# Line recurrences of a two-layer image kernel: even and odd column pairs in two halves of 96 dense rows

## The chip, the cores and the metric

The kernel runs on one core of one Trainium2 chip. The metric is the device time of one launch in microseconds (us). A core has a matrix engine (PE, whose loads of the stationary operand are listed apart as PEld), a vector engine (DVE), a scalar engine (ACT), GpSimd (POOL), a queue engine (SP) and 16 DMA engines. Every engine works its own list of instructions in order and waits on semaphores.

## What is computed

The input x is (2, 48, 512, 512) in float32. Layer 0 adds a convolution with channel attention, layer 1 adds four recurrences over lines of the normalized image:

```python
def step(w, b):
    def f(carry, inp):
        nxt = inp + _conv1d(carry, w, b)      # 48 -> 48 channels, K = 5 taps along the line, padding 2
        return (nxt, nxt)
    return f
_, d_rest = scan(step(down_w, down_b), xs[0], xs[1:])       # D: rows downwards
seq = concatenate([D[Hh - 3::-1], D[Hh - 1:Hh]], 0)
_, u_rest = scan(step(down_w, down_b), D[Hh - 1], seq)      # U: rows upwards
_, r_rest = scan(step(right_w, right_b), ws[0], ws[1:])     # R: columns of U to the right
_, l_rest = scan(step(left_w, left_b), R[Ww - 1], R[Ww - 2::-1])   # L: columns of R to the left
x = x + L
```

Each recurrence has 512 lines, and a line needs the one before it. So there are 4 x 512 = 2,048 dependent steps, each a convolution of 48 channels with 5 taps over 512 places, for a batch of two.

## The kernel before

Layer 0 and the statistics of the second normalization take the first half of the time; the change leaves them alone but for the small preparation of weights in `split_scan_taps`. Then `scans` (L1146) runs the four ways "down", "up", "right", "left" one after the other, and `final_sum` adds the result to x.

**Layout.** The 512 places of a line are taken as 256 pairs. A tile has 112 partitions: the 48 channels of the even places in rows 0 to 47, those of the odd places in rows 64 to 111, and 16 rows of zeros between. The free axis holds 2 batches x 256 pairs = 512 columns (`LP`). The five taps become three 112 x 112 matrices, for the pair before, the pair itself and the pair after; a shift by one pair is a shift of the 512 columns by one, and `hi` and `lo` have an empty column at each end of a batch.

**Precision.** A state is kept as a sum hi + lo of two fp32r tiles, and the taps as scan_high + scan_low. A line needs scan_high x hi, scan_low x hi and scan_high x lo, three shifts each: nine matmuls of 512 columns. The fourth product is left out.

**One line k** (`steps` of each engine):
- the line's input plus bias is written into one of `SLOTS` = 4 PSUM banks ahead of time (`seed`): ACT does it in "down" (two ACTIVATEs, one per batch, L1567) and "right" (L1571, read with a stride of 16 floats), DVE in "up" and "left" (L1472);
- PE adds the three scan_high x hi passes of line k (`high_products`, L1401) and counts `conv_done`;
- ACT casts the bank into `hi` (L1588) and counts `hi_ready`, which PE needs for the next line's first products;
- PE meanwhile adds the three scan_low x hi passes (`low_products`, L1409) and, once `lo` of the line before is there, the three scan_high x lo passes (L1414), and counts `low_done`;
- DVE computes lo = bank - hi (L1483), waiting for `low_done` and for the state two lines back;
- POOL adds hi + lo (L1520) into the tile that goes to memory in "down" and "right", or into a ring of 16 lines in "up" and "left" (`room`); from the ring ACT copies four lines at a time into the transposed layout of the leaving tile (`lay`: L1544 in "up", two copies in most lines, L1538 in "left").

PE's order within a line is high products of line k + 1, then low products of line k. ACT's and DVE's order is written out in their `steps`: the line's own operation, then a seed or copies.

**Transfers.** Groups of T = 16 lines are loaded and stored by SP, double buffered. A load of group g waits until the seeds have read group g - 2 (`consumed`), a store until the states (or the copies out of the ring) of the group are complete. In "down" SP issues all four loads of a group; ACT issues two of the first four. POOL clears the 32 rows between the parities of the first two input tiles (L1523) before the first loads of "down".

## Time and profile before

| | us |
|---|---|
| median of 3 runs | 10,179.8 (10,179.77 to 10,181.08) |
| the profiled execution | 10,184.16 |
| its span, first to last instruction | 10,182.5 |
| PE busy | 9,178.7 (90%) |
| PE weight loads busy | 7,753.5 (76%) |
| DVE busy | 6,163.4 (61%) |
| ACT busy | 6,540.9 (64%) |
| POOL busy | 2,811.9 (28%) |
| granted PE clock, mean over the span | 0.957 of full speed |

Matmuls are pipelined and their records overlap, so that a busy PE need not be one at its peak: the distance from start to start tells more. A row of a timeline gives the start, the length, the engine, the line of the kernel, the operation with what it writes and reads, the shape and the number of instructions merged into it, and in brackets how long the engine had been idle and what ended that. "SPq" and "ACTq" are the issue of transfers.

### The profile page before, as it was taken

What the parts mean: (1) busy time and instruction counts of PE and PEld (TensorE: products, weight loads), DVE (VectorE), ACT (ScalarE), POOL (GpSimd) and SP (SyncE); (2) the same over time, 40 slices, a digit from 0 to 9 for tenths busy, and PEclk for the clock granted to TensorE, in tenths of its full rate; (3) what the DMA queues carried; (4) which work ended last, traced back from release to release, by engine and by line L of the source; (5) the groups of instructions that cost most, each with busy time, mean ns of one, the idle gap of its engine ahead of it and who ended that gap; (6) DMA issues with size and microseconds to landing.
All of it is one profiled execution on the core that took longest, in us unless ns stands there. A gap on an engine that the chain in (4) does not pass through costs nothing. (4 is left out here: it accounts for less than half of the span.)

```text
span 10182.5 us, 167735 instructions
## 1 busy us (share of the span) xinstructions
PE 9178.7 (90%) x53872; PEld 7753.5 (76%) x53872; DVE 6163.4 (61%) x10420; ACT 6540.9 (64%) x10026; POOL 2811.9 (28%) x2287
## 2 busy tenths in 40 slices
PE   3999999999999999999899999999999999999000
PEld 3999999999999998777677777777777777777000
DVE  8888888777777775666633335666433336666323
ACT  2777777777777775444377777888877775555000
POOL 0000000000000000000156665666566656666000
PEclk9999999999999999999999999999999999999555
DMA  8888887666666665999989986777766657777999
GB/s 268 171 166 170 170 169 145 129 132 131 134 135 132 133 135 132 291 291 287 257 182 206 198 206 184 218 218 217 206 223 212 220 180 203 203 202 190 371 433 408
DMA packets 770594, 2101.18 MB, mean 206 GB/s; under 512 B 58976, under 2 KB 633728, under 8 KB 674256
## 3 DMA queue, kind: packets, MB, share of 16 engines
q1 hardware_dynamic: 629824, 1744.21, 67.0%
q0 software_dynamic: 34304, 151.01, 5.8%
q10 hardware_dynamic: 106368, 204.76, 5.6%
q8 instruction: 48, 0.79, 0.0%
q14 instruction: 50, 0.41, 0.0%
HBM read 1344.55 MB, written 754.97 MB: 206 GB/s over the span
## 5 line engine op out<-in xcount | busy, mean ns | idle before, releaser
L1483 DVE TENSOR_TENSOR lo<-scan_ps,hi 112x512 fp32r<-112x512 f32 x2048 | 1416.1, 691 | 2263.0 <-PE scan_ps L1414 1130.7
L1588 ACT CAST hi<-scan_ps 112x512 fp32r<-112x512 f32 x2048 | 1202.9, 587 | 1095.5 <-PE scan_ps L1401 1082.7
L463 PE MATMUL conv_ps<-tap_low,x_high 128*128 128x432 f32 (+2 forms) x6144 | 1904.9, 310 | 0.0
L463 PE MATMUL conv_ps<-tap_high,x_low 128*128 128x432 f32 (+2 forms) x6144 | 1903.6, 310 | 0.0
L463 PE MATMUL conv_ps<-tap_high,x_high 128*128 128x432 f32 (+2 forms) x6144 | 1881.0, 306 | 13.0 <-DVE x_edge L659 7.5
L1401 PE MATMUL scan_ps<-hi,scan_high 112*112 112x512 f32 x6132 | 1777.4, 398 | 40.4 <-ACT hi L1588 33.0
L1414 PE MATMUL scan_ps<-lo,scan_high 112*112 112x512 f32 x6132 | 1769.8, 397 | 0.6
L1409 PE MATMUL scan_ps<-hi,scan_low 112*112 112x512 f32 x6132 | 1768.2, 397 | 0.0
L1520 POOL TENSOR_TENSOR lines<-hi,lo 112x512 f32<-112x512 f32 x1024 | 1323.0, 1292 | 871.4 <-DVE lo L1483 871.4
L1520 POOL TENSOR_TENSOR ring<-hi,lo 112x512 f32<-112x512 f32 x1024 | 1326.2, 1295 | 843.9 <-DVE lo L1483 843.9
L1401 PEld LDWEIGHTS scan_ps<-hi,scan_high 112*112 112x112 f32 x6132 | 1075.4, 176 | 408.6 <-ACT scan_ps L1567 18.0
L1414 PEld LDWEIGHTS scan_ps<-lo,scan_high 112*112 112x112 f32 x6132 | 1077.2, 176 | 365.9 <-DVE lo L1483 3.6
L1409 PEld LDWEIGHTS scan_ps<-hi,scan_low 112*112 112x112 f32 x6132 | 1076.6, 176 | 361.9
L310 ACT ACTIVATE x_high<-raw,negmean 128x512 fp32r<-128x512 f32 x1024 | 1208.1, 1232 | 11.7 <-DMA v_blocks<-xs 6.9
L655 DVE SCALAR_TENSOR_TENSOR x_low<-raw,negmean,x_high 128x512 fp32r<-128x512 f32 x1024 | 1147.3, 1150 | 85.1 <-ACT x_high L310 85.0
L463 PEld LDWEIGHTS conv_ps<-tap_high,x_high 128*128 128x128 f32 x6144 | 1160.8, 189 | 35.4 <-issue 9.1
L463 PEld LDWEIGHTS conv_ps<-tap_high,x_low 128*128 128x128 f32 x6144 | 1164.4, 190 | 18.8
L463 PEld LDWEIGHTS conv_ps<-tap_low,x_high 128*128 128x128 f32 x6144 | 1162.2, 189 | 19.9 <-issue 0.2
L351 ACT COPY xs<-conv_ps 128x288 f32<-128x288 f32 x1024 | 409.4, 400 | 975.2 <-PE conv_ps L469 974.0
L670 DVE TENSOR_TENSOR xs<-conv_ps,xs 128x192 f32<-128x192 f32 x1024 | 365.1, 357 | 657.3 <-ACT vt L352 651.8
L1472 DVE TENSOR_SCALAR scan_ps<-lines,scan_bias 112x512 f32<-112x512 f32 x1021 | 760.6, 745 | 0.0
L1544 ACT COPY lines<-ring 48x512 f32<-48x512 f32 x1024 | 669.4, 654 | 19.3 <-POOL ring L1520 0.9
(145 smaller groups left out, 11670.0 us busy)
## 6 DMA issues: line engine op xcount, KB each, us to landing
raw<-x SPq DMA_DIRECT2D x764, 256.0 KB, 4.9
d_rows<-lines SPq DMA_DIRECT2D x32, 3584.0 KB, 24.3
u_cols<-lines SPq DMA_DIRECT2D x64, 1792.0 KB, 10.6
r_cols<-lines SPq DMA_DIRECT2D x32, 3584.0 KB, 16.6
lines<-u_cols SPq DMA_DIRECT2D x31, 3584.0 KB, 16.4
lines<-r_cols SPq DMA_DIRECT2D x30, 3584.0 KB, 16.6
lines<-d_rows SPq DMA_DIRECT2D x30, 3360.0 KB, 15.5
v_blocks<-xs ACTq DMA_DIRECT2D x128, 768.0 KB, 4.5
```

Of the source, the lines that this page charges most:

```text
L310: ins = nc.scalar.activation(x_high[:, s, k, :, 1:TOK + 1], phases(raw, s, k), ACT.Identity, bias=negmean0[:, 0, b:b + 1], scale=1.0)
L351: nc.scalar.copy(qk_at(i % 2, dy, 0, 3), qk_of(left))
L463: nc.tensor.matmul(bank(dy, side, lo - side, hi - side), xs[at], ws[taps], start=fresh[side], stop=False, skip_group_check=True)
L655: ins = nc.vector.scalar_tensor_tensor(x_low[:, s, k, :, 1:TOK + 1], phases(raw, s, k), negmean0[:, 0, b:b + 1], x_high[:, s, k, :, 1:TOK ...
L1401: last = nc.tensor.matmul(slot(k), w_hi[:, TAPS_OF[way], shift], hi[:, (k - 1) % HIS, :, shift:shift + LP], start=False, stop=False, skip_ ...
L1409: nc.tensor.matmul(slot(k), w_lo[:, TAPS_OF[way], shift], hi[:, (k - 1) % HIS, :, shift:shift + LP], start=False, stop=False, skip_group_c ...
L1414: last = nc.tensor.matmul(slot(k), w_hi[:, TAPS_OF[way], shift], lo[:, (k - 1) % LOS, :, shift:shift + LP], start=False, stop=shift == 2, ...
L1472: ins = nc.vector.tensor_scalar(to, of, b_sb[:, TAPS_OF[way]:TAPS_OF[way] + 1], None, ALU.add)
L1483: nc.vector.tensor_tensor(low_of(k), ps[:, k % SLOTS], high_of(k), ALU.subtract).then_inc(lo_ready, 1)
L1520: nc.gpsimd.tensor_tensor(state(way, s, k), high_of(k), low_of(k), ALU.add).then_inc(state_done, 1)
L1544: return nc.scalar.copy(tile[ODD * r:ODD * r + C, b, h:h + LEAD // 2, :, :, q], rows.rearrange("p t (c m) -> p t c m", c=W // T))
L1588: nc.scalar.copy(high_of(k), ps[:, k % SLOTS]).then_inc(hi_ready, 1)
```

## The change

Even and odd places still lie in one tile, but densely: rows 0 to 47 and 48 to 95 (`SC` = 96). The pairs of a line are now themselves split: even pairs form the half X and odd pairs the half Y of the free axis, 2 batches x 128 pairs (`LQ`) = 256 columns each. The middle tap matrix takes a whole line in one pass for the scan_high x hi product; the neighbours need half passes, since the pair before an even pair is an odd one. Rows 96 to 127 are free: `hi` gets there, in its X half, a copy of rows 32 to 63 of the Y half (made by ACT), and `lo` gets copies of rows 0 to 31 and 64 to 95 of hi's Y half in its Y and X halves (made by DVE, two copies a line). The weight tiles have matching rows of scan_low, so that passes over 128 rows carry part of the scan_low x hi product along with others. A line now has 15 matmuls: 1 of 512 columns and 4 of 256 for the high product, 4 of 256 before the wait for `lo` and 6 of 256 behind it.

Every way is seeded by both engines, DVE batch 1 and ACT batch 0, into 8 PSUM banks. The ring and ACT's copies out of it are gone: POOL writes the leaving tile directly, in "up" in runs of four floats, in "left" one float in every 32. The memsets of rows 32 to 63 go. SP's loads wait for `hi_ready` instead of the seeds, the stores of "up" are four transfers instead of two, and ACT issues half of the loads of "down" (`load_down`). Tensors in memory have 96 rows instead of 112.

```diff
-        scan_high = keep("scan_high", [PP, len(weights), 3, PP], F32R)
-        scan_low = keep("scan_low", [PP, len(weights), 3, PP], F32R)
-        scan_bias = keep("scan_bias", [PP, len(weights)])
+        scan_high = keep("scan_high", [128, len(weights), 4, SC], F32R)
+        scan_low = keep("scan_low", [128, len(weights), 3, SC], F32R)
...
-                        link(nc.vector.tensor_copy(scan_high[:], scan_taps[:]))
-                        nc.vector.tensor_tensor(scan_low[:], scan_taps[:], scan_high[:], ALU.subtract)
+                        rows, spare = slice(0, SC), slice(SC, 128)
+                        nc.vector.tensor_copy(scan_high[rows, :, 3], scan_taps[:, :, 1])
+                        link(nc.vector.tensor_copy(scan_high[rows, :, 0:3], scan_taps[:]))
+                        link(nc.vector.tensor_tensor(scan_low[rows], scan_taps[:], scan_high[rows, :, 0:3], ALU.subtract))
+                        for tile, at, first, shift in ((scan_low, 0, 32, 1), (scan_low, 1, 32, 2), (scan_high, 0, 64, 1),
+                                                       (scan_high, 1, 64, 2), (scan_high, 2, 0, 2), (scan_high, 3, 0, 1)):
+                            nc.vector.tensor_copy(tile[spare, :, at], scan_low[first:first + 32, :, shift])
...
-    LP = W2
-    RING = 16
-    LEAD = 4
+    LQ = W2 // 2
+    ROWS, SPARE = slice(0, SC), slice(SC, 128)
+    X, Y = 0, 1
...
-    DVE_AHEAD = 3
-    HIS, LOS, SLOTS = 4, 2, 4
+    DVE_AHEAD = 4
+    HIS, LOS, SLOTS = 4, 2, 8
...
+    ACT_SEEDS, DVE_SEEDS = 0, 1
...
-    STORES = {"down": 1, "up": 2, "right": 1, "left": 4}
+    STORES = {"down": 1, "up": 4, "right": 1, "left": 4}
...
-        lines = [sb(f"lines{n}", [PP, 2, T * B * LP]) for n in range(2)]
...
-        hi = sb("hi", [PP, HIS, B, LP + 2], F32R)
-        lo = sb("lo", [PP, LOS, B, LP + 2], F32R)
-        ring = sb("ring", [PP, RING, B, LP])
...
+        lines = [sb(f"lines{n}", [SC, 2, T * B * W2]) for n in range(2)]
+        skipped = sb("skipped", [SC, B * W2])
+        hi = sb("hi", [128, HIS, 2, B, LQ + 2], F32R)
+        lo = sb("lo", [128, LOS, 2, B, LQ + 2], F32R)
...
+        banks = ctx.enter_context(nc.psum_tensor("scan_ps", [PP, SLOTS, 2, B, LQ], F32))
+        ps = banks[ROWS]
...
+        def spare_of(tile, x):
+            return tile[SPARE, x, :, 1:LQ + 1]
+        def odd_rows(k, at):
+            return hi[at:at + 128 - SC, k % HIS, Y, :, 1:LQ + 1]
...
-                    sp.wait_ge(seeded[way], seeds0(way) + T * g - T)
+                    sp.wait_ge(hi_ready, states0(way) + T * g - T)
+                def written(way, g):
+                    sp.wait_ge(state_done, states0(way) + T * g + T)
...
                 def store_up(g, s):
-                    for b in range(B):
-                        tile = leaving("up", s).rearrange("p (b c x) -> p b c x", b=B, c=W // T)[:, b]
-                        sp.dma_start(u_cols[:, :, b, bass.ds(g * -NP + NP * (G - 1), NP)].rearrange("c p h t -> p c (h t)"),
-                                     tile).then_inc(stored["up"][s], 16)
+                    for q in range(2):
+                        tile = leaving("up", s)[C * q:C * q + C].rearrange("p (r c n) -> p r c n", r=2, c=W // T)
+                        for r in range(2):
+                            sp.dma_start(u_cols[:, r, :, q, bass.ds(g * -1 + (G - 1), 1)].rearrange("g c u n -> c g (u n)"),
+                                         tile[:, r]).then_inc(stored["up"][s], 16)
...
-                def slot(k):
-                    return ps[:, k % SLOTS]
+                def half(way, k, x, taps, at, of, x_in, shift, rows=ROWS):
+                    return nc.tensor.matmul(ps[:, k % SLOTS, x], taps[rows, TAPS_OF[way], at], of[rows, x_in, :, shift:shift + LQ],
+                                            start=False, stop=False, skip_group_check=True)
...
                 def high_products(way, g, k):
-                    pe.wait_ge(seeded[way], seeds0(way) + T * g + k + 1)
+                    high = hi[:, (k - 1) % HIS]
+                    await_seeds(pe, way, T * g + k + 1)
                     pe.wait_ge(hi_ready, states0(way) + T * g + k)
-                    for shift in range(3):
-                        last = nc.tensor.matmul(slot(k), w_hi[:, TAPS_OF[way], shift], hi[:, (k - 1) % HIS, :, shift:shift + LP],
-                                                start=False, stop=False, skip_group_check=True)
-                    last.then_inc(conv_done, 1)
+                    nc.tensor.matmul(ps[:, k % SLOTS], w_hi[ROWS, TAPS_OF[way], 1], high[ROWS, :, :, 1:LQ + 1],
+                                     start=False, stop=False, skip_group_check=True)
+                    half(way, k, X, w_hi, 0, high, Y, 0)
+                    half(way, k, Y, w_hi, 0, high, X, 1)
+                    half(way, k, X, w_hi, 2, high, Y, 1)
+                    half(way, k, Y, w_hi, 2, high, X, 2).then_inc(conv_done, 1)
                 def low_products(way, g, k):
+                    high, low, every = hi[:, (k - 1) % HIS], lo[:, (k - 1) % LOS], slice(0, 128)
                     pe.wait_ge(hi_ready, states0(way) + T * g + k + 1)
-                    for shift in range(3):
-                        nc.tensor.matmul(slot(k), w_lo[:, TAPS_OF[way], shift], hi[:, (k - 1) % HIS, :, shift:shift + LP],
-                                         start=False, stop=False, skip_group_check=True)
+                    half(way, k, Y, w_lo, 0, high, X, 1, every)
+                    half(way, k, X, w_lo, 0, high, Y, 0)
+                    half(way, k, X, w_lo, 1, high, X, 1, every)
+                    half(way, k, Y, w_lo, 2, high, X, 2)
                     pe.wait_ge(lo_ready, states0(way) + T * g + k)
-                    for shift in range(3):
-                        last = nc.tensor.matmul(slot(k), w_hi[:, TAPS_OF[way], shift], lo[:, (k - 1) % LOS, :, shift:shift + LP],
-                                                start=False, stop=shift == 2, skip_group_check=True)
-                    last.then_inc(low_done, 1)
+                    half(way, k, Y, w_hi, 0, low, X, 1, every)
+                    half(way, k, X, w_hi, 0, low, Y, 0)
+                    half(way, k, X, w_hi, 1, low, X, 1, every)
+                    half(way, k, Y, w_hi, 3, low, Y, 1, every)
+                    half(way, k, X, w_hi, 2, low, Y, 1, every)
+                    half(way, k, Y, w_hi, 2, low, X, 2).then_inc(low_done, 1)
...
                     slot_free(v, way, g - s, k, kept)
-                    to, of = ps[:, k % SLOTS], line(way, s, k % T, kept)
-                    if bare:
+                    b = DVE_SEEDS
+                    to, of = ps[:, k % SLOTS, :, b], line(way, s, k % T, b, kept)
+                    if way == "down":
+                        shift = gn1_bias if bare else down_shift
+                        ins = nc.vector.tensor_scalar(to, of, gn1_scale[:, b:b + 1], shift[:, b:b + 1], ALU.mult, ALU.add)
+                    elif bare:
                         ins = nc.vector.tensor_copy(to, of)
                     else:
                         ins = nc.vector.tensor_scalar(to, of, b_sb[:, TAPS_OF[way]:TAPS_OF[way] + 1], None, ALU.add)
-                    ins.then_inc(dve_seeded, 1)
+                    ins.then_inc(dve_seeded[way], 1)
                 def steps(way, g, first=False, last=False):
                     for k in range(2 * T):
                         done = states0(way) + T * g + k
                         v.wait_ge(hi_ready, done + 1)
+                        nc.vector.tensor_copy(spare_of(lo[:, k % LOS], Y), odd_rows(k, 0))
+                        nc.vector.tensor_copy(spare_of(lo[:, k % LOS], X), odd_rows(k, 64))
                         if not (first and k == 0):
                             v.wait_ge(low_done, convs0(way) + T * g + k)
                         if not (way == "down" and first and k < LOS):
                             v.wait_ge(state_done, done - LOS + 1)
                         nc.vector.tensor_tensor(low_of(k), ps[:, k % SLOTS], high_of(k), ALU.subtract).then_inc(lo_ready, 1)
-                        if way in laid:
...
+                        ahead = k + DVE_AHEAD
+                        if ahead < 2 * T:
+                            seed(way, g + ahead // T, ahead // T, ahead, first)
+                        elif not last:
+                            seed(way, g + ahead // T, ahead // T - 2, ahead - 2 * T)
...
+                def state(way, s, k):
+                    high, low = high_of(k), low_of(k)
+                    if way == "up":
+                        r, h = (T - 1 - k % T) % 2, (T - 1 - k % T) // 2
+                        tile = leaving(way, s).rearrange("p (r c h x b m) -> p r h (x b) c m", r=2, c=W // T, h=NP, x=2, b=B)
+                        return (tile[:, r, h], high.rearrange("p x b (c m) -> p (x b) c m", c=W // T),
+                                low.rearrange("p x b (c m) -> p (x b) c m", c=W // T))
+                    if way == "left":
+                        tile = leaving(way, s).rearrange("p (b m x t) -> p x b m t", b=B, x=2, t=T)
+                        return tile[..., T - 1 - k % T], high, low
+                    return leaving(way, s).rearrange("p (t x b m) -> p t x b m", t=T, x=2, b=B)[:, k % T], high, low
...
-                        nc.gpsimd.tensor_tensor(state(way, s, k), high_of(k), low_of(k), ALU.add).then_inc(state_done, 1)
-                for s in range(2):
-                    nc.gpsimd.memset(arriving("down", s)[32:64], 0.0).then_inc(between_clear, 1)
...
                     arrived(act, way, g, s, k % T, kept)
-                    slot_free(act, way, g - s, k, kept)
-                    to, of = ps[:, k % SLOTS], line(way, s, k % T, kept)
+                    act.wait_ge(dve_seeded[way], T * (g - s) + k + 1)
+                    b = ACT_SEEDS
+                    to, of = ps[:, k % SLOTS, :, b], line(way, s, k % T, b, kept)
...
-                        for b in range(B):
-                            ins = nc.scalar.activation(to[:, b], of[:, b], ACT.Identity, bias=shift[:, b:b + 1], scale=gn1_scale[:, b:b + 1])
+                        ins = nc.scalar.activation(to, of, ACT.Identity, bias=shift[:, b:b + 1], scale=gn1_scale[:, b:b + 1])
...
-                def behind(way, g, k):
...
-                        if way in laid:
-                            if not (first and k < LEAD + LAG):
-                                behind(way, g, k)
-                        else:
-                            ahead = k + ACT_AHEAD
-                            if ahead < 2 * T:
-                                seed(way, g + ahead // T, ahead // T, ahead, first)
-                            elif not last:
-                                seed(way, g + ahead // T, ahead // T - 2, ahead - 2 * T)
...
+                        if way == "down" and k == LAG and not first:
+                            await_seeds(act, way, T * g)
+                            load_down(act, g + 1, 1, 1)
+                        if way == "down" and k == T + LAG and not last:
+                            await_seeds(act, way, T * g + T)
+                            load_down(act, g + 2, 0, 1)
+                        ahead = k + ACT_AHEAD
+                        if ahead < 2 * T:
+                            seed(way, g + ahead // T, ahead // T, ahead, first)
+                        elif not last:
+                            seed(way, g + ahead // T, ahead // T - 2, ahead - 2 * T)
+                        act.wait_ge(hi_ready, states0(way) + T * g + k + 1)
+                        nc.scalar.copy(spare_of(hi[:, k % HIS], X), odd_rows(k, 32))
```

## Rows read from the trace of the kernel before

**Rows 1.** The page's part 1: busy us (share) and instructions of each engine.

```profile
PE 9178.7 (90%) x53872; PEld 7753.5 (76%) x53872; DVE 6163.4 (61%) x10420; ACT 6540.9 (64%) x10026; POOL 2811.9 (28%) x2287
```

**Rows 2.** Windows: one stretch of each way. Busy of PE, PEld, DVE, ACT, POOL; PEclk; DMA; GB/s.

```profile
5101.00:6136.00 1035.00, 1035.00 (x4416) 773.65 (x4415) 339.30 (x491) 757.31 (x1470) 633.00 (x490) 1.00 0.89 198
...
```

**Rows 3.** Timeline of "right", one line and the start of the next.

```profile
7500.13 0.69 DVE L1483 TENSOR_TENSOR lo<-scan_ps,hi 112x512 fp32r<-112x512 f32 x1 [1.42 <-PE scan_ps L1414]
...
7500.58 0.86 PE L1409 MATMUL scan_ps<-hi,scan_low 112*112 112x512 f32 x3
7500.78 0.59 ACT L1588 CAST hi<-scan_ps 112x512 fp32r<-112x512 f32 x1 [0.47 <-PE scan_ps L1401]
7500.97 1.29 POOL L1520 TENSOR_TENSOR lines<-hi,lo 112x512 f32<-112x512 f32 x1 [0.81 <-DVE lo L1483]
...
7502.69 0.86 PE L1409 MATMUL scan_ps<-hi,scan_low 112*112 112x512 f32 x3
```

**Rows 4.** Timeline of PE in the first layer: 288 and 144 columns wide.

```profile
2500.83 0.29 PE L463 MATMUL conv_ps<-tap_low,x_high 128*128 128x288 f32 x1
2500.96 0.29 PE L463 MATMUL conv_ps<-tap_high,x_low 128*128 128x288 f32 x1
...
2501.16 0.28 PE L463 MATMUL conv_ps<-tap_low,x_high 128*128 128x144 f32 x1
2501.27 0.27 PE L463 MATMUL conv_ps<-tap_high,x_low 128*128 128x144 f32 x1
```

**Rows 5.** Groups by line: busy us, mean ns | idle before, releaser.

```profile
L1472 DVE TENSOR_SCALAR scan_ps<-lines,scan_bias 112x512 f32<-112x512 f32 x1021 | 760.6, 745 | 0.0
...
L1544 ACT COPY lines<-ring 48x512 f32<-48x512 f32 x1024 | 669.4, 654 | 19.3 <-POOL ring L1520 0.9
L1571 ACT ACTIVATE scan_ps<-lines,scan_bias 112x512 f32<-112x512 f32 x511 | 593.2, 1161 | 0.0
L1567 ACT ACTIVATE scan_ps<-lines,down_shift,gn_scale 112x256 f32<-112x256 f32 x1022 | 543.3, 567 | 0.0
...
L1569 ACT COPY scan_ps<-lines 112x512 f32<-112x512 f32 x1 | 1.0, 1014 | 2.6 <-DMA lines<-lines 2.6
```

**Rows 6.** Timeline of SP's queue: loads of "down", a store of "up".

```profile
5226.96 2.08 SPq L1263 DMA_DIRECT2D lines<-x_scan  x4
...
6498.77 4.82 SPq L1302 DMA_DIRECT2D u_cols<-lines  x1
```

**Rows 7.** Timelines at 3,961 us and 5,067 us: DVE beside POOL's memsets.

```profile
3961.54 6.91 POOL L865 MEMSET res<- 112x8192 f32 x1
...
3964.49 0.17 DVE L99 TENSOR_TENSOR rnorm<-rnorm,norm 96x16 f32<-96x16 f32 x1
...
3964.90 3.58 DVE L101 TENSOR_SCALAR rnorm<-rnorm 96x16 f32<-96x16 f32 x1
...
5067.13 13.80 POOL L1523 MEMSET lines<- 32x8192 f32 x2 [12.70 <-POOLq L811]
5067.17 6.90 DVE L1449 COPY gn_mean<-x_mv 112x2 f32<-112x2 f32 x1 [3.96 <-PEq L811]
```

**Rows 8.** Groups: DVE from SBUF to SBUF, one input.

```profile
L647 DVE COPY raw<-mean 32x512 f32<-32x512 f32 x2 | 0.8, 420 | 0.1
...
L597 DVE CAST edge_high<-edge_f 128x288 fp32r<-128x288 f32 x2 | 0.6, 302 | 0.0
```

**Rows 9.** Timeline of "up": DVE's two operations of a line and POOL's.

```profile
6499.68 0.69 DVE L1483 TENSOR_TENSOR lo<-scan_ps,hi 112x512 fp32r<-112x512 f32 x1 [0.75 <-issue]
...
6500.29 0.74 DVE L1472 TENSOR_SCALAR scan_ps<-lines,scan_bias 112x512 f32<-112x512 f32 x1
...
6500.52 1.29 POOL L1520 TENSOR_TENSOR ring<-hi,lo 112x512 f32<-112x512 f32 x1 [0.81 <-DVE lo L1483]
```

**Rows 10.** Timeline of PE in the first lines of "down", at the lower clock.

```profile
5100.25 1.48 PE L1414 MATMUL scan_ps<-lo,scan_high 112*112 112x512 f32 x3
...
5101.53 1.41 PE L1401 MATMUL scan_ps<-hi,scan_high 112*112 112x512 f32 x3
```

More of the change, by code:

```diff
@@ L24 @@
 PP = ODD + C
+SC = 2 * C
 T = 16
@@ L1186, in scans @@
         hi_ready, state_done, lo_ready = sem("hi_ready"), sem("state_done"), sem("lo_ready")
-        act_seeded, dve_seeded = sem("act_seeded"), sem("dve_seeded")
-        seeded = {"down": act_seeded, "up": dve_seeded, "right": act_seeded, "left": dve_seeded}
+        act_seeded = {way: sem(f"{way}_act_seeded") for way in WAYS}
+        dve_seeded = {way: sem(f"{way}_dve_seeded") for way in WAYS}
         loaded = {way: [sem(f"{way}_loaded{s}") for s in range(2)] for way in WAYS}
         stored = {way: [sem(f"{way}_stored{s}") for s in range(2)] for way in WAYS}
-        laid = {way: sem(f"{way}_laid") for way in ("up", "left")}
         skipped_in, first_right = sem("skipped_in"), sem("first_right")
@@ L1254, in slot_free, with await_seeds @@
                 engine.wait_ge(lo_ready, states0(way) + T * g + k - SLOTS + 1)
+        def await_seeds(engine, way, n):
+            engine.wait_ge(act_seeded[way], n)
+            engine.wait_ge(dve_seeded[way], n)
         def high_free(engine, way, g, k, first):
@@ L1273, in load_up @@
                 def load_up(g, s, last=False):
-                    rows = arriving("up", s).rearrange("p (t x) -> p t x", t=T)
-                    here = one(d_rows, g * -1 + (G - 1)).rearrange("g p t b n -> (g p) t (b n)")
-                    before = one(d_rows, G - 1 if last else g * -1 + (G - 2)).rearrange("g p t b n -> (g p) t (b n)")
+                    rows = arriving("up", s).rearrange("p (t n) -> p t n", t=T)
+                    here = one(d_rows, g * -1 + (G - 1)).rearrange("g p t n -> (g p) t n")
+                    before = one(d_rows, G - 1 if last else g * -1 + (G - 2)).rearrange("g p t n -> (g p) t n")
                     sp.dma_start(rows[:, 1:T], here[:, 0:T - 1]).then_inc(loaded["up"][s], 16)
@@ L1334, in _ @@
                         consumed("down", 2 * i + s)
-                        for q in range(2):
-                            load_down(sp, 2 * i + s, s, q)
+                        load_down(sp, 2 * i + s, s, 0)
                         store_rows("down", d_rows, 2 * i + s - 2, s)
@@ L1503, in room @@
                 def room(way, g, s, k, kept):
-                    if way in laid:
-                        if k % LEAD == 0 and not (kept and T * s + k < RING):
-                            pool.wait_ge(laid[way], (T // LEAD) * g + k // LEAD - (RING // LEAD - 1))
-                    elif k == 0:
+                    if k == 0:
                         if not kept:
@@ L1547, in lay_block @@
-                def lay_block(way, g, s, k, at, of):
-                    n_ops = 8 if way == "up" else 4
-                    if at == 0 and k == 0 and not (isinstance(g, int) and g < 2):
-                        act.wait_ge(stored[way][s], 8 * STORES[way] * (g - s))
-                    if at == 0:
-                        act.wait_ge(state_done, states0(way) + T * g + k + LEAD)
-                    for j in range((n_ops * at + of - 1) // of, (n_ops * (at + 1) + of - 1) // of):
-                        ins = lay(way, s, k, j)
-                        if j == n_ops - 1:
-                            ins.then_inc(laid[way], 1)
@@ L1571, in seed @@
                         ins = nc.scalar.activation(to, of, ACT.Identity, bias=b_sb[:, TAPS_OF[way]:TAPS_OF[way] + 1], scale=1.0)
-                    ins.then_inc(act_seeded, 1)
-                def behind(way, g, k):
-                    at = k - LAG - LEAD - (k - LAG) % LEAD
-                    gone, s = (g + at // T, at // T) if at >= 0 else (g - 1, 1)
-                    for half in range(2):
-                        lay_block(way, gone, s, at % T, 2 * ((k - LAG) % LEAD) + half, 2 * LEAD)
+                    ins.then_inc(act_seeded[way], 1)
                 def steps(way, g, first=False, last=False):
@@ L1583, in steps @@
                         if first and k == 0:
[L1584 removed]
+                            await_seeds(act, way, 1)
                         else:
@@ L1607, in _ @@
                 for way in WAYS:
-                    if way not in laid:
-                        if way == "right":
-                            act.wait_ge(first_right, 16 * FIRST_RIGHT)
-                        for k in range(ACT_AHEAD):
-                            seed(way, 0, 0, k, True, k == 0)
+                    if way == "right":
+                        act.wait_ge(first_right, 16 * FIRST_RIGHT)
+                    elif way in ("up", "left"):
+                        act.wait_ge(state_done, states0(way))
+                    for k in range(ACT_AHEAD):
+                        seed(way, 0, 0, k, True, k == 0)
                     steps(way, 0, first=True)
@@ L1616, in _ @@
                     steps(way, G - 2, last=True)
-                    if way in laid:
-                        for k in range(2 * T, 2 * T + LEAD + LAG):
-                            behind(way, G - 2, k)
 def final_sum(nc, sem, x1_scan, l_rows, out):
```

153 lines of the change are left out of this document (67 added, 86 removed).

## The prediction

> **What bounds the kernel now.** I read the engine totals first, then busy time by stage, then one line of a recurrence in order of time, then the waits. The totals [rows 1] have PE at 90%; matmuls overlap in the records, so the stages are needed. The four recurrences run one after the other, and in each PE is busy throughout at a granted clock of 0.99 to 1.00, the 2.4 GHz level (the row of the first; the other three read the same to within 2%) [rows 2]. There are 2,048 lines. In the timeline of "right" the three L1409 passes of one line start at 7500.58 and those of the next at 7502.69: **2.11 us a line**, nine passes, 0.234 us each, with no gap at the three places where PE waits [rows 3]. 2,048 x 2.11 = 4,321 us, the stage's length. In the same rows each other engine waits within the line: ACT 0.47 us, DVE 1.42, POOL 0.81. So PE's stream sets the line. What follows, the final sum, is not touched.
>
> **What PE gains.** Per line 9 full passes (18 halves) become 1 full and 14 half passes: 16 halves in 15 matmuls. No 256-wide matmul stands in the trace; its neighbours do. In the first layer 288-wide passes start 0.13 us apart and 144-wide ones 0.11 us apart, both with 128-column weights [rows 4]. So the interval follows the width (288 wide 0.13, 512 wide 0.234: both 0.457 ns a column) until about 0.11 us, where the weight load takes over. 256 x 0.457 = 0.117 us is above that floor, and the new weights have 96 columns, not 128. I take 0.117 (ends 0.117 and 0.13); the line is 16 x 0.117 = **1.875 us** of PE, 0.235 less. The whole saving, if nothing else ends later: 0.235 x 2,048 = 481 us.
>
> **What ACT gets.** The cast stays, 0.59 us [rows 3]. In "down" its two seeds of 256 columns become one, 0.567. In "up" and "left" the copies out of the ring go (L1544, 0.654 each, two in most lines of "up" [rows 5]) and a seed comes; in "right" a seed of 512 halves. The strided 512-wide seed took 1.161 [rows 5], so a strided 256-wide one lies between 0.567 and 0.72. The new copy into the 32 spare rows of hi costs between 0.33, half of the 512-wide copy L1544, and 0.567, the 256-wide seed with its two scalars; I take 0.40. Sum 1.56 to 1.71 us, under 1.875: no cost, though only 0.2 us covers it. ACT also issues two transfers in 16 lines of "down", which SP did in 0.52 us each (four in 2.08) [rows 6]: 1 us a group, in ACT's idle time if the line is as long as I forecast, otherwise at most 30 us over the 32 groups.
>
> **What DVE gets.** Its subtraction stays at 0.69 [rows 3]. A seed of 512 columns took 0.745 [rows 5]; with 0.17 us of it fixed (the small L99 [rows 7]) the half is 0.46. In "down" and "right" it is new. New in every line are two copies, 32 rows x 256, SBUF to SBUF. Rows for such copies: 288 wide in 0.302, 512 wide in 0.420 [rows 8], so 0.5 ns a column and 256 wide 0.286 each. That is twice the subtraction's and the seed's pace (the seed: 0.575 us for 512, 1.1 ns a column). Alone, DVE has 0.69 + 0.46 + 0.57 = 1.72 us, again under 1.875.
>
> **The step that decides.** Those two copies stand on DVE's queue between the seed and the next subtraction, and POOL's addition of the line (1.29 us) begins 0.15 us after each subtraction ends (7500.82 to 7500.97 [rows 3]) and lasts until 1.44 us after it. Twice the trace of before shows a plain one-source f32 DVE operation from SBUF to SBUF beginning while POOL runs [rows 7]. L1449 copies two columns: 6.903 us, from 5067.17 to 5074.07, while POOL's first memset (half of 13.80) ends at 5074.03. L101 scales 16 columns: 3.58 us from 3964.90, ending at 3968.48, while the memset L865 ends at 3968.45. L99, of the same size but with two inputs, ran just before it beside the same memset in 0.17, and in the recurrence the seed, which writes PSUM, runs at 0.74 beside POOL's addition [rows 9]. So the fast copy from SBUF to SBUF waits for POOL and the others don't. That is how I take the new copies: blocked until POOL's addition ends.
> Then the line is a loop DVE, POOL, DVE: lag 0.15 + POOL 1.29 + copies + subtraction 0.69. A blocked operation ended 0.03 to 0.04 us after POOL (its start-up is past), so the first copy needs 0.03 + 0.13 (256 columns at 0.5 ns) = 0.16 after POOL; the second 0.286; hand-over 0.03: 0.15 + 1.29 + 0.16 + 0.286 + 0.03 + 0.69 = **2.60 us**. Lower end 2.415, with each of the two later operations beginning 0.08 us before the last one ends, as seed and subtraction do [rows 9]; upper end 2.80, where the first copy has its full 0.286 behind POOL with 0.04 gaps. Behind a subtraction PE has a lag (POOL's was 0.15), 6 + 6 + 4 half passes, 0.15 + 0.70 + 0.70 + 0.47 = 2.02 us, and then waits some 0.6 us for the next remainder.
> The Trainium skill ("SBUF — State Buffer", "Who interferes with whom") has the rule: a DVE copy in a two-port mode and a GpSimd instruction hold one shared pair of SBUF ports exclusively, and the second one fully blocks. The trace agrees for memsets (the two rows above); beside a POOL addition no row of before has such a copy. Without the rule the sum would be rival 1's.
>
> **Small terms.** POOL's writes in "up" come in runs of four floats, in "left" one every 128 bytes. No POOL row is strided. On ACT a copy with a 64-byte stride took 1.014 us (L1569) against 0.654 (L1544) [rows 5], 1.55 times, and against the cast's 0.59 1.7 times; POOL by that 2.0 to 2.14. POOL spends 2.5 ns an element (1.29 / 512) where the cast spends 1.15, so it has time for a slow write and I take nothing and keep +0.85 us x 512 = +435 us for "left" as an end. The two memsets ahead of "down" go: the first load waits for one of them, 6.9 us [rows 7], so -7 us. SP issues four stores in a group of "up" instead of two (4.82 us for one [rows 6]): at most 19 us in a group of over 30, and the same bytes less 1/7. Its loads now wait for the cast, not the seed, two to three lines later, and still come 12 lines, over 22 us, ahead of the first seed that reads them. The six copies that fill the spare weight rows come once, at the start; by the 0.302 of a 288-wide one [rows 8] they are 2 us.
>
> **Sum.** (2.60 - 2.11) x 2,048 = +1,004; -7; on the profiled execution's 10,184.2: 11,181. The median of the runs is 4 us lower; I forecast **11,180 us**. Own range of this case: 2.415 gives +625, 10,800; 2.80 gives +1,413, 11,590, with the strided end 12,025.
>
> **Rivals.**
> 1. *The copies don't wait* (POOL's additions, unlike memsets, leave the ports free, or the order differs). PE stays the bound at 1.875 us: 10,180 - 481 - 7 + 30 = **9,720 us**. For it: each engine fits, DVE with 0.15 us to spare. Against it: both blocked rows. It ends on the other side, and decides from the point where the two copies together take less than 0.72 us (1.875 - 0.69 - 0.46) beside POOL. Chance 0.15.
> 2. *The copies go at half the pace, like the seed, and don't wait*: about 0.42 each (0.286 + 0.133); DVE then is the bound at 0.69 + 0.46 + 0.84 = 1.99 us. 10,180 - 0.12 x 2,048 = **9,930 us**. Against it: both rows at 0.5 ns a column, a cast into fp32r among them [rows 8]. Chance 0.10.
> 3. *No block, but strided writes slow POOL* to 2.29 us a line in "up" and "left": -0.235 x 1,024 + 0.18 x 1,024 - 7 = **10,116 us**. Chance 0.03.
> 4. *Block, and the PE clock falls* because PE pauses 0.6 us each line. At 1.2 GHz a full pass takes 0.427 us (L1414 at 5100.25 to L1401 at 5101.53 [rows 10]); 16 halves are 3.4 us, **12,840 us**. Against it: the waits are short. Chance 0.04.
>
> **How the numbers follow.** Forecast 0.68; rivals 0.15, 0.10, 0.03, 0.04. Slower by over 0.2% (20 us, about what a measurement tells from no change): 0.68 + 0.04 = 0.72. Faster: 0.15 + 0.10 + 0.02 = 0.27; same 0.01. The range from 9,700 to 11,900 takes in the forecast but for its strided tail (0.63) and rivals 1 to 3 (0.28).
>
> **What would show it.** The two new DVE copies: if blocked, the first averages near 1.2 us and ends within 0.2 of POOL's end, the second 0.29; the L1401 group waits for lo about 0.6 us a line, and the period is 2.6 in all four ways. If the copies average 0.29 beside POOL and PE starts half passes 0.117 us apart without gaps, rival 1 is right. If they average 0.42, rival 2. POOL's mean by way (1.29 or near 2) settles the strided writes, the granted clock rival 4. A 96-row pass at over 0.13 us, or the first copy ending long before POOL, would make the prediction wrong.

## The result and the profile after

The changed kernel takes **11,161.3 us** (median of 4 runs, 11,159.0 to 11,166.9) against 10,180.4 of the kernel before (also 4 runs): 1.0964 times as long, interval 1.0945 to 1.0983. It is 981 us slower. The forecast was 11,180 us. The profiled execution took 11,163.2 us, 979 more than that of before.

The engine totals of the changed kernel's page, in the columns of [rows 1]:

```profile
PE 9281.8 (83%) x66142; PEld 8312.0 (74%) x66142; DVE 9261.1 (83%) x15547; ACT 6486.3 (58%) x11050; POOL 2802.6 (25%) x2285
```

DVE grew from 6,163 to 9,261 us of busy time, POOL stayed as it was. Busy time by stretch, one of each of the four ways ("down", "up", "right", "left"), in the columns of [rows 2]:

```profile
5200.00:6200.00 1000.00, 834.03 (x5793) 712.91 (x5792) 977.30 (x1545) 605.43 (x1159) 499.39 (x387) 1.00 0.55 151
6700.00:7700.00 1000.00, 833.10 (x5794) 713.40 (x5795) 977.47 (x1547) 564.09 (x1159) 498.99 (x387) 1.00 0.62 151
7900.00:8900.00 1000.00, 830.96 (x5790) 711.95 (x5790) 977.63 (x1545) 662.94 (x1158) 499.57 (x386) 1.00 0.52 151
9200.00:10300.00 1100.00, 912.93 (x6351) 781.53 (x6350) 1075.36 (x1695) 618.72 (x1271) 551.31 (x424) 1.00 0.62 151
```

POOL makes one addition a line: 387 in 1,000 us is a line every **2.59 us**, the same in all four ways, where before it was 2.11 [rows 3]. (2.59 - 2.11) x 2,048 = 983 us, which is the whole difference. PE is no longer busy throughout (83%), the granted clock stays 1.00, and DVE shows 98%. That figure alone would read as "DVE has too much work". The timeline of one line in "down" shows otherwise (start, duration, engine, line, operation, and in brackets the idle time before it and what ended it; the two copies are L1504 and L1505, the subtraction L1510, the seed L1493, POOL's addition L1560):

```profile
5501.19 0.69 DVE L1510 TENSOR_TENSOR lo<-scan_ps,hi 96x512 fp32r<-96x512 f32 x1
5501.80 0.53 DVE L1493 TENSOR_SCALAR scan_ps<-lines,gn_scale,down_shift 96x256 f32<-96x256 f32 x1
...
5501.94 0.97 PE L1404 MATMUL scan_ps<-lo,scan_high 128*96 128x256 f32 x6 [0.44 <-DVE lo L1510]
5502.02 1.30 POOL L1560 TENSOR_TENSOR lines<-hi,lo 96x512 f32<-96x512 f32 x1 [1.30 <-DVE lo L1510]
5502.37 1.11 DVE L1504 CAST lo<-hi 32x256 fp32r<-32x256 f32 x1
...
5503.49 0.29 DVE L1505 CAST lo<-hi 32x256 fp32r<-32x256 f32 x1
...
5503.79 0.69 DVE L1510 TENSOR_TENSOR lo<-scan_ps,hi 96x512 fp32r<-96x512 f32 x1
```

Two copies of the same form, one straight after the other, take 1.11 and 0.29 us. POOL's addition runs from 5502.02 to 5503.32; the first copy starts inside it and ends at 5503.48, 0.16 after it. The next subtraction starts at 5503.79, 2.60 us after the last. It is so in nearly every line: 2,030 of the 2,048 first copies begin during POOL's addition, and they end 0.15 us behind it on average (nearly all between 0.14 and 0.16). The groups by line (busy us, mean ns of one | idle before, releaser) agree:

```profile
L1560 POOL TENSOR_TENSOR lines<-hi,lo 96x512 f32<-96x512 f32 x2048 | 2653.2, 1295 | 2708.5 <-DVE lo L1510 2704.5 <-ACT hi L1591 4.0
L1504 DVE CAST lo<-hi 32x256 fp32r<-32x256 f32 x2048 | 2237.5, 1093 | 67.4 <-ACT hi L1591 3.8
L1404 PE MATMUL scan_ps<-lo,scan_high 128*96 128x256 f32 x8176 | 1717.3, 301 | 881.5 <-DVE lo L1510 881.5
L1510 DVE TENSOR_TENSOR lo<-scan_ps,hi 96x512 fp32r<-96x512 f32 x2048 | 1406.3, 687 | 39.9 <-PE scan_ps L1404 12.3
L1604 ACT CAST hi<-hi 32x256 fp32r<-32x256 f32 x2048 | 826.0, 403 | 50.7
L1505 DVE CAST lo<-hi 32x256 fp32r<-32x256 f32 x2048 | 602.8, 294 | 27.8
```

Three engines hand the work round: POOL's idle time is ended by the subtraction (2,704 us), PE's too (881 us), and DVE shows almost none, because a blocked copy counts as busy.

### The profile page after: what moved, and what is told of

Same layout as the page of the kernel before. It is cut to its first block and busy times, and to the rows that moved or that the text cites. A ratio compares the mean times of both kernels' runs of the same rounds, so it can differ in the third digit from the quotient of the medians.

```text
span 11161.6 us, 201419 instructions
## 1 busy us (share of the span) xinstructions
PE 9281.8 (83%) x66142; PEld 8312.0 (74%) x66142; DVE 9261.1 (83%) x15547; ACT 6486.3 (58%) x11050; POOL 2802.6 (25%) x2285
## 5 line engine op out<-in xcount | busy, mean ns | idle before, releaser
L1560 POOL TENSOR_TENSOR lines<-hi,lo 96x512 f32<-96x512 f32 x2048 | 2653.2, 1295 | 2708.5 <-DVE lo L1510 2704.5
L1404 PE MATMUL scan_ps<-lo,scan_high 128*96 128x256 f32 x12264 | 1965.6, 295 | 881.5 <-DVE lo L1510 881.5
L1404 PEld LDWEIGHTS scan_ps<-lo,scan_high 128*96 128x96 f32 x12264 | 1480.7, 162 | 1355.9 <-DVE lo L1510 1354.9
L1504 DVE CAST lo<-hi 32x256 fp32r<-32x256 f32 x2048 | 2237.5, 1093 | 67.4 <-ACT hi L1591 3.8
L1591 ACT CAST hi<-scan_ps 96x512 fp32r<-96x512 f32 x2048 | 1193.1, 583 | 595.9 <-PE scan_ps L1404 587.4
L1510 DVE TENSOR_TENSOR lo<-scan_ps,hi 96x512 fp32r<-96x512 f32 x2048 | 1406.3, 687 | 39.9 <-PE scan_ps L1404 12.3
L1404 PE MATMUL scan_ps<-hi,scan_low 128*96 128x256 f32 x8176 | 1315.1, 282 | 0.0
L1404 PE MATMUL scan_ps<-hi,scan_high 96*96 96x256 f32 x8176 | 1313.4, 282 | 0.0
L1404 PEld LDWEIGHTS scan_ps<-hi,scan_high 96*96 96x96 f32 x8176 | 1152.5, 162 | 155.4
L1404 PEld LDWEIGHTS scan_ps<-hi,scan_low 128*96 128x96 f32 x8176 | 1072.8, 163 | 0.0
```

Source lines behind the costliest of these rows:

```text
L1404: return nc.tensor.matmul(ps[:, k % SLOTS, x], taps[rows, TAPS_OF[way], at], of[rows, x_in, :, shift:shift + LQ], start=False, stop=False, ...
L1504: nc.vector.tensor_copy(spare_of(lo[:, k % LOS], Y), odd_rows(k, 0))
L1510: nc.vector.tensor_tensor(low_of(k), ps[:, k % SLOTS], high_of(k), ALU.subtract).then_inc(lo_ready, 1)
L1560: nc.gpsimd.tensor_tensor(to, high, low, ALU.add).then_inc(state_done, 1)
L1591: nc.scalar.copy(high_of(k), ps[:, k % SLOTS]).then_inc(hi_ready, 1)
```

## The experiments

The theory: a fast DVE copy from SBUF to SBUF and POOL's addition shut each other out. The rival: DVE simply has too much work, or the copy is long for a reason of its own. The kernel before took 10,181 us beside them (14 runs, 10,175 to 10,190). Experiments 1 to 5 are one execution each, 6 to 8 four; the differences from it that the argument rests on are 97 us or more. Experiments 1, 3, 4 and 6 were set down first, 2, 5, 7 and 8 with their results known. In the recorded expectations "e1" is experiment 6, and "as measured without copies" is experiment 1.

**1. The two copies left out.** This kernel leaves out the part of the product of the low weights and hi that the spare rows carry.

```diff
-                        nc.vector.tensor_copy(spare_of(lo[:, k % LOS], Y), odd_rows(k, 0))
-                        nc.vector.tensor_copy(spare_of(lo[:, k % LOS], X), odd_rows(k, 64))
```

> Both DVE copies are left out, so lo has zeros in its 32 spare rows and a part of the scan_low x hi product is missing. This prices the pair: both theories expect it to give back what the pair costs. DVE then has 0.69 + 0.47 us and PE is the bound at 16 x 0.117 = 1.875 us a line: 9,720 us. If half passes are dearer than 0.117 us, this run shows it: at 0.13 us a line is 2.08 us and the time 10,120 us.

Measured: 9,823.9 us. The copies cost 1,337 us altogether. Without them PE sets the pace; its timeline in "right":

```profile
7800.72 0.88 PE L1404 MATMUL scan_ps<-lo,scan_high 128*96 128x256 f32 x6
...
7801.44 0.40 PE L1412 MATMUL scan_ps<-hi,scan_high 96*96 96x512 f32 x1
...
7801.68 0.64 PE L1404 MATMUL scan_ps<-hi,scan_high 96*96 96x256 f32 x4
...
7802.15 0.64 PE L1404 MATMUL scan_ps<-hi,scan_low 128*96 128x256 f32 x4
...
7802.63 0.65 PE L1404 MATMUL scan_ps<-lo,scan_high 128*96 128x256 f32 x4
```

Six halves in 0.72, one full pass in 0.24, four halves in 0.47 and four in 0.48: a half takes **0.119 us** and this line 1.91; over each way the median is 1.92. So the change without its two copies gives 10,181 - 9,824 = 357 us, not the 481 of the working.

**2. One of the two copies left out** (the X rows' copy, so half of that part of the product is missing). If the length of the first is the wait, the second costs only its own 0.29.

> The changed kernel without the second DVE copy (the X half of lo's spare rows stays zero, a part of the scan_low x hi product is missing), the first one in its place. Block theory: the wait stays and only the 0.29 us go: 2.59 - 0.29 = 2.30 us a line, 10,570 us, still slower than before. Work theory, by which DVE's true work is 0.69 + 0.29 + 0.47 us: no more than PE's 1.925 us, 9,830 us.

Measured: 10,543.4 us, 618 less than the changed kernel (0.30 x 2,048). The remaining copy's group:

```profile
L1504 DVE CAST lo<-hi 32x256 fp32r<-32x256 f32 x2048 | 2234.6, 1091 | 68.8 <-ACT hi L1590 5.0
```

It keeps its 1.09 us. DVE's own work is now 0.69 + 0.29 + 0.47 = 1.45 us (0.29 for a copy that doesn't wait), well under PE's 1.92, and still a line takes 2.29. Excess work is out.

**3. The copies slower but with an operand in PSUM.** The same values arrive by adding a block of zeros that stands in PSUM:

```diff
+        nothing = banks[SPARE, SLOTS - 1, 0]
...
-                        nc.vector.tensor_copy(spare_of(lo[:, k % LOS], Y), odd_rows(k, 0))
-                        nc.vector.tensor_copy(spare_of(lo[:, k % LOS], X), odd_rows(k, 64))
+                        nc.vector.tensor_tensor(spare_of(lo[:, k % LOS], Y), odd_rows(k, 0), nothing, ALU.add)
+                        nc.vector.tensor_tensor(spare_of(lo[:, k % LOS], X), odd_rows(k, 64), nothing, ALU.add)
```

> The two copies are made as additions of a zero block in PSUM (one operand in SBUF, one in PSUM), in the same place of DVE's queue, so the same values move at half the pace, as the subtraction does beside POOL. Block theory: only the fast copy from SBUF to SBUF waits for POOL, so these take 0.42 us each without a wait, DVE has 0.69 + 0.47 + 0.84 = 2.00 us less some overlap, and the time falls to 9,800 to 9,980 us although the instructions are slower. Work theory: each is 0.13 us longer, so 11,160 + 0.26 x 2,048 = 11,700 us.

Measured: **10,084.3 us**. Timeline in "up":

```profile
6501.51 1.29 POOL L1562 TENSOR_TENSOR lines<-hi,lo 96x512 f32<-96x512 f32 x1 [0.70 <-DVE lo L1512]
...
6501.79 0.43 DVE L1506 TENSOR_TENSOR lo<-hi,scan_ps 32x256 fp32r<-32x256 f32 x1
...
6502.23 0.43 DVE L1507 TENSOR_TENSOR lo<-hi,scan_ps 32x256 fp32r<-32x256 f32 x1
```

Both run beside POOL's addition at 0.43 us each. Operations that take half as long again as a free copy made the kernel 1,077 us faster. They read the same rows of hi and write the same rows of lo as the copies did, so the use of the same tiles is not what made the copies wait. The run doesn't tell the operand in PSUM from the second input that came with it: both were changed at once. It came 104 us above the expected span: I had counted overlaps between DVE's operations that aren't there, and the strided seed of "right" at the price of the others (below). A line takes 2.00 us in "up" and "left", 2.09 in "down" and 2.19 in "right".

**4. POOL's addition made twice,** first into a scratch tile. Only a wait for POOL makes DVE's copies longer by this.

```diff
+                        nc.gpsimd.tensor_tensor(again[:, k % 4], high_of(k), low_of(k), ALU.add)
                         nc.gpsimd.tensor_tensor(to, high, low, ALU.add).then_inc(state_done, 1)
```

> POOL makes every addition twice, the first time into a scratch tile. Block theory: POOL's time stands in the line's loop, so the line grows by all of it, 1.29 us, to 3.9 us, and the time to about 13,800 us; the first copy then averages 2.4 us. Work theory (POOL is beside the path; DVE waits only for the state two lines back): POOL becomes the bound at 2 x 1.29 + 0.15 = 2.75 us, at most 11,490 us.

Measured: 13,163.0 us, 2,002 more than the changed kernel, 0.98 a line. POOL is busy 2.62 of 3.57 us, so it isn't the bound itself. The timeline:

```profile
6503.12 1.29 POOL L1561 TENSOR_TENSOR again<-hi,lo 96x512 f32<-96x512 f32 x1 [1.00 <-DVE lo L1511]
6503.47 1.10 DVE L1505 CAST lo<-hi 32x256 fp32r<-32x256 f32 x1
...
6504.38 1.33 POOL L1562 TENSOR_TENSOR lines<-hi,lo 96x512 f32<-96x512 f32 x1
...
6504.58 1.28 DVE L1506 CAST lo<-hi 32x256 fp32r<-32x256 f32 x1
```

The first copy slipped in between the two additions and ended at 6504.57; the second then waited for the second addition (to 6505.71) and ended 0.15 after it. So the loop grew by POOL's 1.29 less the 0.3 us of a copy that no longer stood behind POOL, which is the 0.98. I had expected both copies behind the last addition, 1.29 a line.

**5. The kernel before with two such copies added** ahead of each subtraction, into a scratch tile that nobody reads. All else is as before, with its nine full passes.

```diff
+                        for q in range(2):
+                            nc.vector.tensor_copy(extra[96:128, k % 4, q], hi[64:96, k % HIS, :, 1 + 128 * q:129 + 128 * q])
```

> The kernel before, with nothing of the change but two DVE copies of 32 rows x 256 columns from hi into a scratch tile, ahead of each subtraction. Block theory: DVE, POOL and the copies form the same loop as in the changed kernel, 0.15 + 1.29 + 0.16 + 0.29 + 0.69 = 2.6 us a line instead of 2.11, about 11,160 us, in all four ways. Work theory: DVE has 0.69 + 0.58 us in down and right and 2.0 us in up and left, always under the 2.11 us of PE, so the time stays within 1% of 10,180 us.

Measured: 10,802.3 us, 622 us slower than before although DVE idled 1.42 us a line in "right" [rows 3]. It missed the expectation, which had 2.6 us a line in all four ways: a line takes 2.33 us in "down" and "right" and 2.50 in "up" and "left", against 2.12 on average before. In "down" DVE has only 0.69 + 0.58 us of work of its own, so work can't be the cause there. A pair of copies, in "down" and in "up":

```profile
5501.03 1.59 DVE L1481 CAST extra<-hi 32x256 fp32r<-32x256 f32 x2
...
5501.15 1.32 POOL L1523 TENSOR_TENSOR lines<-hi,lo 112x512 f32<-112x512 f32 x1 [1.01 <-ACT hi L1591]
...
6500.45 1.30 POOL L1523 TENSOR_TENSOR ring<-hi,lo 112x512 f32<-112x512 f32 x1 [1.20 <-DVE lo L1486]
6501.00 1.10 DVE L1481 CAST extra<-hi 32x256 fp32r<-32x256 f32 x2
```

In "down" the copies begin 0.12 us ahead of POOL: the first goes through and only the second waits. In "up" a seed stands between and both come behind. One copy waits in either case, so the block is there without any other part of the change; its size depends on what stands just ahead of the copies.

**6. The copies straight behind the subtraction,** ahead of the seed, for the line after. They could get in before POOL.

```diff
-                        v.wait_ge(hi_ready, done + 1)
-                        nc.vector.tensor_copy(spare_of(lo[:, k % LOS], Y), odd_rows(k, 0))
-                        nc.vector.tensor_copy(spare_of(lo[:, k % LOS], X), odd_rows(k, 64))
...
                         nc.vector.tensor_tensor(low_of(k), ps[:, k % SLOTS], high_of(k), ALU.subtract).then_inc(lo_ready, 1)
+                        if not (last and k == 2 * T - 1):
+                            v.wait_ge(hi_ready, done + 2)
+                            spares(k + 1)
```

> DVE's two copies for line k + 1 are moved to right behind the subtraction of line k, ahead of the seed, so that they start before POOL's addition of line k can. Block theory (the copies wait because POOL's addition has begun): no copy waits, both take 0.29 us, POOL's addition waits instead and starts some 0.55 us behind the subtraction, which nobody notices (0.55 + 1.29 is under a line); PE becomes the bound at about 1.88 us a line, 9,720 to 9,850 us. If POOL gets in between the two copies, the second one waits: 2.9 us a line, about 11,800 us. Work theory (the line is long because DVE has more to do): same work, so 11,160 us.

Measured: **11,785.8 us** (4 runs, ratio 1.1575, 1.1556 to 1.1595), worse than the change itself, and the second case of the expectation. The first case, in which no copy waits, is wrong.

```profile
6500.41 0.69 DVE L1514 TENSOR_TENSOR lo<-scan_ps,hi 96x512 fp32r<-96x512 f32 x1
...
6501.13 0.29 DVE L1501 CAST lo<-hi 32x256 fp32r<-32x256 f32 x1
...
6501.24 1.31 POOL L1567 TENSOR_TENSOR lines<-hi,lo 96x512 f32<-96x512 f32 x1 [1.57 <-DVE lo L1514]
6501.43 1.28 DVE L1502 CAST lo<-hi 32x256 fp32r<-32x256 f32 x1
...
6502.73 0.54 DVE L1493 TENSOR_SCALAR scan_ps<-lines,gn_scale,down_shift 96x256 f32<-96x256 f32 x1
```

The first copy wins, then POOL takes its turn ahead of the second, which ends 0.16 after POOL (6502.55). And now the seed stands behind the blocked copy as well, where in the changed kernel it ran beside POOL: 0.54 of seed for 0.29 of copy, 2.89 a line in "down" (2.84 in "up" and "left", 3.03 in "right"). An order on DVE's queue alone doesn't settle who gets in.

**7. The same, with the second copy by a PSUM operand.**

```diff
+                    nc.vector.tensor_copy(spare_of(lo[:, k % LOS], Y), odd_rows(k, 0))
+                    nc.vector.tensor_tensor(spare_of(lo[:, k % LOS], X), odd_rows(k, 64), nothing, ALU.add)
```

> The order of e1 (copies for line k + 1 right behind the subtraction), but the second copy has its zero operand in PSUM and so does not wait for POOL. Block theory: the first copy, 0.29 us, starts before POOL's addition and only moves that by 0.2 us; the second takes 0.43 us beside POOL; DVE has 0.69 + 0.29 + 0.43 + 0.47 = 1.88 us less overlaps of about 0.2, so PE is the bound with 1.925 us a line (as measured without copies) and the time is 9,830 to 9,900 us, faster than both kernels. Against it: if a slow copy that starts beside POOL's addition waits too, 2.9 us a line as in e1, 11,790 us.

Measured: 10,045.0 us (4 runs, ratio 0.9870, 0.9853 to 0.9886). Timeline in "up":

```profile
6501.15 0.69 DVE L1516 TENSOR_TENSOR lo<-scan_ps,hi 96x512 fp32r<-96x512 f32 x1
...
6501.87 0.29 DVE L1503 CAST lo<-hi 32x256 fp32r<-32x256 f32 x1
6501.98 1.32 POOL L1569 TENSOR_TENSOR lines<-hi,lo 96x512 f32<-96x512 f32 x1 [0.66 <-DVE lo L1516]
6502.17 0.43 DVE L1504 TENSOR_TENSOR lo<-hi,scan_ps 32x256 fp32r<-32x256 f32 x1
6502.61 0.48 DVE L1499 TENSOR_SCALAR scan_ps<-lines,scan_bias 96x256 f32<-96x256 f32 x1
6503.13 0.69 DVE L1516 TENSOR_TENSOR lo<-scan_ps,hi 96x512 fp32r<-96x512 f32 x1
```

The two take 0.289 and 0.427 us on average and neither waits, but DVE's four steps follow each other without overlap and it becomes the bound, above the expected span: 1.98 us a line in "up" and "left", 2.06 in "down", 2.17 in "right".

**8. The same order, both copies fast, and POOL made to wait** for the second of them:

```diff
+                    nc.vector.tensor_copy(spare_of(lo[:, k % LOS], X), odd_rows(k, 64)).then_inc(spared, 1)
...
+                        if not (last and k == 2 * T - 1):
+                            pool.wait_ge(spared, states0(way) + T * g + k + 2)
```

> The order of e1 with both fast copies, and POOL's addition of line k waits (a semaphore) until the two copies that follow the subtraction of line k are done, so POOL can no longer get in between. Block theory: copies 0.5 us, lag 0.1 to 0.15, addition 1.29 us, and the next first copy starts behind POOL's end: 1.85 to 2.05 us a line, PE's 1.925 us at the least, 9,830 to 10,080 us. If the wait in e1 had another cause than the order of the two engines, 11,790 us as there.

Measured: **9,882.0 us** (4 runs, 9,880.8 to 9,884.5; ratio 0.9708, 0.9692 to 0.9724). It beats the kernel before by 298 us and the change by 1,279.

```profile
6502.14 0.69 DVE L1515 TENSOR_TENSOR lo<-scan_ps,hi 96x512 fp32r<-96x512 f32 x1
...
6502.85 0.29 DVE L1502 CAST lo<-hi 32x256 fp32r<-32x256 f32 x1
...
6503.16 0.29 DVE L1503 CAST lo<-hi 32x256 fp32r<-32x256 f32 x1
6503.48 0.48 DVE L1498 TENSOR_SCALAR scan_ps<-lines,scan_bias 96x256 f32<-96x256 f32 x1
6503.52 1.29 POOL L1570 TENSOR_TENSOR lines<-hi,lo 96x512 f32<-96x512 f32 x1 [0.64 <-DVE lo L1503]
```

POOL starts 0.7 us after the subtraction's end instead of 0.14. That costs nothing, since the loop from addition to copies to addition, 0.07 + 1.29 + 0.15 + 0.02 + 0.29 = 1.82 us by these rows (an estimate; 0.15 is what a copy needs behind POOL), is now shorter than PE's line, by 0.1 us. The median line takes 1.92 us in "up" and "left", as in experiment 1, and 1.94 in "down". "Right" is longer: a line there takes 2.05 (starts of the subtraction at 7800.82 and 7802.87), because its strided DVE seed takes 0.69 and DVE becomes the bound. On average a line of "right" takes 2.07 us against 1.94 in experiment 1, 69 us in all; "down" is 9 us shorter than there, and the two kernels are 58 apart.

## Why the prediction was right, and where it was off

**The deciding step held.** "The fast copy from SBUF to SBUF waits for POOL" was drawn from two rows beside memsets [rows 7]. Experiments 2 to 5 show it for POOL's addition: the wait stays when DVE's load goes down, goes when the copy becomes an addition with a PSUM operand, grows with POOL's work, and appears in the kernel before. The other half of that sentence, "and the others don't", is shown for operations that read or write PSUM (the subtraction, the seed, experiment 3) alone; no run has a DVE operation with two inputs in SBUF beside an addition of POOL. The rule of the Trainium skill ("SBUF — State Buffer", "Who interferes with whom") said that they block each other, and the runs agree in both directions: 1.09 us for a copy that needs 0.29, and 1.44 for an addition that needs 1.295 where the copy came first (the last section has the rows). Experiment 3 agrees with its page "VectorE: DVE Perf Modes", section "Why PSUM operands drop a tier", by which an f32 operation with a PSUM operand gets no two-port mode: 0.427 us instead of 0.288, and no wait.

**The sum of the line held.** Term by term, forecast and timeline: lag 0.15 and 0.14; POOL 1.29 and 1.30; first copy behind POOL 0.16 and 0.16; second 0.286 and 0.29; gaps 0.03 and 0.02; subtraction 0.69 and 0.69. 2.60 against 2.60. The mean over the ways is a little shorter, (11,163 - 10,184) / 2,048 = 0.478 more than 2.11, so 2.59.

**PE.** "Waits some 0.6 us" for the remainder: the timeline has 0.44 on the matmul's own row and the group 881.5 / 2,048 = 0.43. The modelled ends of matmuls reach into the wait; a line of 2.59 with 1.91 of passes leaves 0.68. The half pass was taken as 0.117 us from the 288-wide neighbour and measures 0.119. Since PE isn't the bound, that changes nothing in the forecast, but it was too good for rival 1. Experiment 1 comes near that rival (it has no copies at all), at 9,824 instead of 9,720 us. Its median line takes 1.918 us (1.925 in "right") instead of 1.875, which explains 92 us of the 104. ACT's issue of two loads in each group of "down", put at 30 us at most, makes one line in 16 longer there by 0.3 to 1.4 us, 26 us in all.

**ACT.** The spare copy, 0.40 in the working, took 0.403. Strided 256-wide seeds were put at 0.567 to 0.72; in "right" they take 0.73 in the changed kernel and up to 0.75 in the others. It had slack, as said.

**DVE.** The seed of 0.46 measures 0.47 in "up" and 0.535 in "down". That its strided read in "right" makes it 0.67 to 0.69 was not in the working at all: the price of strides was taken up for ACT and POOL and left out for DVE. Behind a blocked copy it cost nothing, since it runs beside POOL. With the block gone it is what bounds "right" (experiment 8), and rival 1, with "0.15 us to spare" on DVE, would have been short there: 0.69 + 0.57 + 0.69 = 1.95 us of work without the gaps, over PE's 1.875.

**POOL's strided writes** were taken as nothing, with +435 us for "left" kept as an end. The nothing was right: 424 additions took 551.31 us in the "left" window, 1.30 each, and 1.29 in the others. Rival 3 is out, and so is rival 4 by the clock of 1.00. The memsets' -7 us was nearer 4: the first subtraction of "down" starts at 5,091.5 us instead of 5,095.1. Rival 2's pace of 0.42 is that of experiment 3 (0.427), not of the copies.

## What to carry to other kernels

A fast DVE copy from SBUF to SBUF beside a long POOL operation costs what is left of POOL's operation, and if POOL waits for DVE in turn, the two add up into the line: look for two equal DVE operations of which one takes four times as long, and for its end just behind POOL's. Where POOL has slack, make it wait by a semaphore until the copies are through, since an order on DVE's queue alone lets it slip in between them. A slower form of the copy, an addition with an operand in PSUM, needs no such order and was faster than the blocked copy too; it is the one to try where POOL has no slack, which no run here tests. A busy share of 98% may be a wait in disguise.

## What the runs showed of the hardware that I had not expected

- Two copies in a row on DVE, 0.02 us apart, don't hold POOL off: in experiment 6 POOL got in between them in nearly every line (means 0.288 and 1.281 us). In experiment 4 a copy got in between two additions of POOL in the same way.
- The wait goes both ways, and the one that waits needs less behind the other's end than it needs alone. A copy behind POOL ends 0.15 us after POOL's end, of the 0.29 that it needs alone. An addition that begins with 0.17 to 0.19 us of a fast copy left takes 1.32 to 1.33 us instead of 1.295 (experiments 4, 6 and 7), which looks like no wait. But where 0.28 us were left it took 1.44, and in all these cases it ends 1.12 to 1.18 us after the copy's end. In the changed kernel, in "left":

```profile
9229.58 0.29 DVE L1504 CAST lo<-hi 32x256 fp32r<-32x256 f32 x1
...
9229.59 1.44 POOL L1560 TENSOR_TENSOR lines<-hi,lo 96x512 f32<-96x512 f32 x1 [1.58 <-DVE lo L1510]
9229.88 1.30 DVE L1505 CAST lo<-hi 32x256 fp32r<-32x256 f32 x1
```

In experiment 3 an addition that began with 0.42 us of the slower form left took its 1.30:

```profile
8429.59 0.43 DVE L1506 TENSOR_TENSOR lo<-hi,scan_ps 32x256 fp32r<-32x256 f32 x1
8429.59 1.30 POOL L1562 TENSOR_TENSOR lines<-hi,lo 96x512 f32<-96x512 f32 x1 [0.98 <-ACT hi L1593]
```

- Only the seed overlapped the operation ahead of it on DVE, by 0.08 us behind the subtraction. Everything else keeps a gap of 0.01 to 0.04. With the copies between subtraction and seed the sum of the means is therefore a lower bound for DVE's loop (experiment 8, "right": 1.95 of work, 2.05 a line); with the seed straight behind the subtraction the overlap and the gaps nearly cancel (experiment 3, "up": 2.015 and 2.00).
- POOL's addition takes 1.30 us with its output 128 bytes apart, as with its output together. A read of 256 columns with that stride takes DVE 0.67 to 0.69 us instead of 0.47 to 0.48.
